# Routing terms and group deviations held in accumulator banks, image edges cleared in pairs: attention and conditional convolution on one core

## The chip, the cores and the metric

The kernel runs on one core of one Trainium2 chip. The metric is device microseconds of one execution; the time given is the median of several runs. The engines are named as in the profile: PE (TensorE: matrix products and transposes into accumulator banks, PSUM), DVE (VectorE), ACT (ScalarE), POOL (GpSimd) and SP (SyncE, which issues all DMAs). Each works through its own list in order and waits for the others by semaphores. SBUF is the memory of ordinary tensors.

## What is computed

For each of 16 images of 128 channels and 32 x 32 pixels, in float32:

```
x = x + attention(groupnorm(x))       # 4 heads of 32, softmax over d for q, over n for k
y = groupnorm(x)                      # 32 groups of 4 channels
pooled = mean of y over 4 x 4 cells                      # (128, 16)
r = relu(rconv_w . pooled + rconv_b)                     # 16 x 16 = 256 routing terms
g = sigmoid(relu(fc_w . r + fc_b))                       # 3 experts x 128 input channels
w = sum over k of g[k] * expert_weight[k]                # a filter of this image's own
out = x + conv3x3(y, w)                                  # padding of 1
```

## The kernel before

One image takes the whole 128 partitions as channels; the work of six images overlaps as a pipeline. Time goes in steps t, one per image: `run_steps` (line 333) runs steps -1 to 8 and 15 to 20 written out, and 9 to 14 as a loop of two steps. Each engine has a function `step` with its order of parts written by hand; `do(part, t, p, age)` calls a part for image t - age, `turn` the same for the group statistics, where one turn serves the first norm of image j and the second norm of image j - 3 together (`GAP = 3`, two columns). Buffers with index p alternate between even and odd images.

The parts that the change and the prediction touch, in the order of one image's flow:

- Group statistics, tensors of two columns. DVE's bn_aggr gives mean and variance per channel (`meanvar`). PE's `group_means` (L1211) averages the means over groups into `ps_stat`, a bank of 512 columns. DVE's `means` (L824) stores the negated mean (`nmean`), `differences` (L829) adds it to the channel mean (`dev`), `squared_differences` (L836) squares it (`dev_sq`), `spreads` (L843) adds the variance (`spread`). PE's `group_variances` (L1216) averages that, DVE's `variances` (L850) reads it back, POOL takes the power -0.5.
- DVE's `context_mask` (L955), `mix_start` (L949, `mix_base`) and `mix_evacuate` (L964, `mix`) stand behind `spreads`; PE's `outputs` (L1289) needs `mix`.
- Routing. POOL multiplies the pooled values by `rconv_t` (L534). PE's `routing` (L1302) sums them over channels into columns 0 to 255 of `ps_stat`. DVE's `route_bias` (L1032) adds the bias and stores `route_y` in SBUF, column 256 of which is a constant one; `route_sums` (L1043) makes, per expert, the relu of `route_y` times a row of `fc`, summed. Then `route_relu` (L1051), the gates, `filters_second` and `filters_third` (L1082, L1089) mix the expert filters into `w_full`.
- ACT rounds `w_full` to `w_hi` (L700), POOL computes the rest `w_lo` (L544); so too `img_hi`/`img_lo` for pixels. Each tap of the convolution (L1357) makes three products, hi x hi, hi x lo and lo x hi.
- SP copies the images by one column to left and right (L402 to L406). POOL's `image_edges` (L548) waits for all four copies and clears the column that wrapped around, by one instruction for each of the four, before `filters_low` (`w_lo`).
- POOL's `normalise1` (L492) writes `x`, `low1` (L499) `x_lo`, `x_scale` (L511) scales `x_nt`.
- PE's `keep_busy` (L1309) puts products whose result is not used (fillers, L1318, into columns 256 to 511 of `ps_stat`) into steps 1 to 3.

`ps_stat` is shared, so PE waits before it writes there: `group_means` and `keep_busy` wait until the routing terms of an earlier image were taken out (`route_y_done`). DVE's `step` sets the order of all this:

```
turn(means, t, p, 0)
do(k_sums, t, p, 2)
turn(differences, t, p, 0)
do(memory_scale, t, p, 2)
turn(squared_differences, t, p, 0)
```

Of the kernel before, what the change touches and what calls it, by code (L numbers as in the profile page):

```python
# [25 lines left out]
def attention_condconv_kernel(  # L26
# [38 lines left out]
    with ctx:  # L65
# [12 lines left out]
        zeros = sb("zeros", [128, H])  # L78
# [34 lines left out]
        dev_sq = sb("dev_sq", [128, 2])  # L113
# [49 lines left out]
        route_y = sb("route_y", [128, RF + 1])  # L163
# [15 lines left out]
        left_hi = [sb(f"left_hi{p}", [128, H, W], F32R) for p in range(2)]  # L179
        left_lo = [sb(f"left_lo{p}", [128, H, W], F32R) for p in range(2)]  # L180
        right_hi = [sb(f"right_hi{p}", [128, H, W], F32R) for p in range(2)]
        right_lo = [sb(f"right_lo{p}", [128, H, W], F32R) for p in range(2)]
# [11 lines left out]
        ps_stat = psum("ps_stat", [128, 512])  # L194

# [177 lines left out]
        def _(sp):  # L373
# [22 lines left out]
            def flat(img):  # L396
                return img[:, :, :].bitcast(F32).rearrange("p h w -> p (h w)")

            def shift_images(b, p):

                sp.wait_ge(img_hi_done, b + 1)
                sp.dma_start(flat(left_hi[p])[:, 1:N], flat(img_hi[p])[:, 0:N - 1]).then_inc(shifted[p], 16)  # L402
                sp.dma_start(flat(right_hi[p])[:, 0:N - 1], flat(img_hi[p])[:, 1:N]).then_inc(shifted[p], 16)
                sp.wait_ge(img_lo_done, b + 1)
                sp.dma_start(flat(left_lo[p])[:, 1:N], flat(img_lo[p])[:, 0:N - 1]).then_inc(shifted[p], 16)
                sp.dma_start(flat(right_lo[p])[:, 0:N - 1], flat(img_lo[p])[:, 1:N]).then_inc(shifted[p], 16)  # L406
# [35 lines left out]
        def _(pool):  # L442
# [7 lines left out]
            nc.gpsimd.memset(route_y[:, RF:RF + 1], 1.0)  # L450
# [97 lines left out]
            def image_edges(b, p):  # L548
                pool.wait_ge(shifted[p], 32 * (b - p) + 64)
                for img, column in ((left_hi, 0), (left_lo, 0), (right_hi, W - 1), (right_lo, W - 1)):  # L550
                    last = nc.gpsimd.tensor_tensor(img[p][:, :, column:column + 1], zeros[:, :].unsqueeze(2), zeros[:, :].unsqueeze(2), ALU.add)  # L551
                last.then_inc(edges_done, 1)
# [215 lines left out]
        def _(dve):  # L768
            v = nc.vector
            def constants():  # L770
# [10 lines left out]
                v.tensor_copy(memv_t[:, :], ps_att[0:MEM, 128:256])  # L781
# [13 lines left out]
            def memory_mix():  # L795
                dve.wait_ge(setup_pe, 5)
                v.tensor_copy(mem_mix[:, :], ps_att[:, 128:256]).then_inc(setup_dve, 1)
# [28 lines left out]
            def differences(j, p):  # L826
                dve.wait_ge(nmean_done, j + 1)
# [642 lines left out]
```

## Time and profile before

| | us |
|---|---|
| median of 3 runs | 441.21 (437.83 to 441.52) |
| profiled execution | 440.93 |
| its span, first to last instruction | 439.2 |
| PE busy | 414.9 (94%) |
| DVE busy | 359.6 (82%) |
| ACT busy | 303.1 (69%) |
| POOL busy | 262.4 (60%) |

All durations below come from the one profiled execution, taken by the hardware's profiler. PE is matrix products, PEld the loading of their weights, which overlaps them. Products are pipelined and their ends are modelled, so a busy PE is not a PE at its peak. A row of a timeline begins with the start (us from the start of the span) and the duration; `x16` is the count, and in brackets stand the idle time ahead of the first and who ended it. Durations of neighbouring rows overlap a little, since an engine takes up an instruction before the last one has ended. Waits are inferred from semaphore events; "issue" is time without a wait that the profile shows.

### The profile page before, as it was taken

To read this page: it belongs to the slowest core of one execution; us is meant where nothing else is said; L and a number is where in the kernel's file an instruction comes from. 1 tells how busy PE (TensorE), PEld (TensorE's weight loads), DVE (VectorE), ACT (ScalarE), POOL (GpSimd) and SP (SyncE) were. 2 spreads that over 40 slices of the span, in tenths; PEclk is the share of its full clock that TensorE was granted. 3 is DMA by queue.
4 is the path that set the end of the run, shared out by engine and by line. 5 is a ranking of instruction groups with operands and counts; after the bars stand their busy time and mean duration, and the time that the engine had idled before them with its cause. 6 is when DMAs were issued, how large, how long until landed. Compare 5 with 4: busy or idle time off the path is not lost.

```text
span 439.2 us, 8966 instructions
## 1 busy us (share of the span) xinstructions
PE 414.9 (94%) x2575; PEld 360.5 (82%) x2575; DVE 359.6 (82%) x778; ACT 303.1 (69%) x942; POOL 262.4 (60%) x245
## 2 busy tenths in 40 slices
PE   6888798999999999999999999999999999999987
PEld 5887687978888788979898888879798988778777
DVE  4574989798998989898989999898989798997540
ACT  2586685769695887868695959778686968654131
POOL 4646465749394957768494948576584849252330
PEclk8699998999999999999999999999999999999999
DMA  6420224324435151626253351606262422424331
GB/s 191 182 98 2 96 98 147 143 95 171 166 128 209 65 229 43 242 96 241 96 198 140 126 208 57 261 16 239 95 239 96 180 108 96 193 96 193 142 147 48
DMA packets 19078, 61.64 MB, mean 140 GB/s; under 512 B 3025, under 2 KB 4321, under 8 KB 19041
## 3 DMA queue, kind: packets, MB, share of 16 engines
q1 hardware_dynamic: 19040, 61.21, 37.0%
q8 instruction: 16, 0.26, 0.2%
q14 instruction: 22, 0.17, 0.1%
HBM read 19.29 MB, written 8.39 MB: 63 GB/s over the span
## 4 chain that ended last, share of the span: by engine, by line
PE 42%; DVE 22%; issue 16%; ACT 13%; POOL 3%; DMA 3%; DVEq 1%; ACTq 0%; SPq 0%
PE ps_conv L1357 15%; PE ps_y L1289 6%; PE ps_att L1257 5%; DVE w_full L1089 4%; ACT expert_raw L694 4%; DVE q_exp L912 3%; DMA xa<-in_x_dram 3%; DVE route_terms L1043 3%; PE ps_y L1279 3%; POOL w_lo L544 2%; ACT qk L608 2%; ACT squares L581 2%; PE ps_qkv L1238 2%; ACT x_hi L598 2%; PE ps_qkv L1239 2%
## 5 line engine op out<-in xcount | busy, mean ns | idle before, releaser
L608 ACT ACTIVATE qk<-ps_qkv,scale 128x256 f32<-128x256 f32 x128 | 54.3, 470 | 8.0 <-PE ps_qkv L1240 4.3
L700 ACT ACTIVATE w_hi<-w_full 128x1152 fp32r<-128x1152 f32 x16 | 18.7, 1168 | 54.7 <-DVE w_full L1095 54.7
L551 POOL TENSOR_TENSOR left_hi<-zeros 128x32 fp32r<-128x32 f32 x16 | 8.5, 529 | 79.8 <-DMA right_lo<-img_lo 79.8
L544 POOL TENSOR_TENSOR w_lo<-w_full,w_hi 128x1152 fp32r<-128x1152 f32 x16 | 42.7, 2670 | 12.9 <-ACT w_hi L700 8.0
L499 POOL TENSOR_TENSOR x_lo<-x,x_hi 128x1024 fp32r<-128x1024 f32 x16 | 38.4, 2397 | 14.1 <-ACT x_hi L598 14.1
L1238 PE MATMUL ps_qkv<-wqk_hi,x_hi 128*128 128x256 f32 x128 | 41.5, 324 | 1.8 <-ACT qk L608 1.8
L525 POOL TENSOR_TENSOR scale<-ssq,minus_half 128x8 f32<-128x8 f32 x16 | 26.2, 1638 | 28.4 <-DVE ssq L970 28.4
L667 ACT ACTIVATE y_scaled<-ps_y 128x128 f32<-128x128 f32 x128 | 33.3, 292 | 12.0 <-PE ps_y L1289 12.0
L1357 PE MATMUL ps_conv<-img_hi,w_hi 128*128 128x512 f32 (+1 forms) x96 | 37.4, 404 | 3.7 <-POOL w_lo L544 2.1
L1357 PE MATMUL ps_conv<-left_lo,w_hi 128*128 128x512 f32 (+2 forms) x96 | 40.6, 424 | 0.0
L1357 PE MATMUL ps_conv<-right_hi,w_hi 128*128 128x512 f32 (+2 forms) x96 | 38.0, 397 | 0.0
L1357 PE MATMUL ps_conv<-right_hi,w_lo 128*128 128x512 f32 (+2 forms) x96 | 38.0, 396 | 0.0
L1357 PE MATMUL ps_conv<-left_hi,w_hi 128*128 128x512 f32 (+2 forms) x96 | 37.2, 388 | 0.0
L1357 PE MATMUL ps_conv<-left_hi,w_lo 128*128 128x512 f32 (+2 forms) x96 | 37.0, 387 | 0.0
L1357 PE MATMUL ps_conv<-right_lo,w_hi 128*128 128x512 f32 (+2 forms) x96 | 37.0, 386 | 0.0
L1239 PE MATMUL ps_qkv<-wqk_lo,x_hi 128*128 128x256 f32 x128 | 36.6, 286 | 0.0
L1240 PE MATMUL ps_qkv<-wqk_hi,x_lo 128*128 128x256 f32 x128 | 36.5, 285 | 0.0
L1357 PE MATMUL ps_conv<-img_hi,w_lo 128*128 128x512 f32 (+1 forms) x96 | 36.2, 388 | 0.0
L1357 PE MATMUL ps_conv<-img_lo,w_hi 128*128 128x512 f32 (+1 forms) x96 | 35.7, 386 | 0.0
L1257 PEld LDWEIGHTS ps_att<-x_nt,k_exp 128*128 128x128 f32 x256 | 30.3, 190 | 6.4 <-ACT k_exp L634 6.0
L1257 PE MATMUL ps_att<-x_nt,k_exp 128*128 128x130 f32 x256 | 32.3, 278 | 2.7 <-ACT k_exp L634 2.1
L581 ACT ACTIVATE squares<-ps_qkv 128x128 f32<-128x128 f32 x128 | 33.3, 282 | 0.8 <-PE ps_qkv L1223 0.8
(176 smaller groups left out, 1342.5 us busy)
## 6 DMA issues: line engine op xcount, KB each, us to landing
xa<-in_x_dram SPq DMA_DIRECT2D x16, 512.0 KB, 4.0
xb<-in_x_dram SPq DMA_DIRECT2D x16, 512.0 KB, 4.7
left_hi<-img_hi SPq DMA_DIRECT2D x16, 511.5 KB, 3.0
right_hi<-img_hi SPq DMA_DIRECT2D x16, 511.5 KB, 4.1
left_lo<-img_lo SPq DMA_DIRECT2D x16, 511.5 KB, 2.9
right_lo<-img_lo SPq DMA_DIRECT2D x16, 511.5 KB, 3.7
out_dram<-expert_raw SPq DMA_DIRECT2D x15, 512.0 KB, 2.9
expert_raw<-_conv_expert_weight_dram SPq DMA_DIRECT2D x1, 1728.0 KB, 9.1
```

What stands on the lines that cost most here:

```text
L499: nc.gpsimd.tensor_tensor(x1_lo[:, :], x1[:, :], x1_hi[:, :].bitcast(F32), ALU.subtract).then_inc(x1_lo_done, 1)
L525: nc.gpsimd.tensor_tensor(scale2[:, :], ssq2[:, :], minus_half[:, :], ALU.pow).then_inc(scale2_done, 1)
L544: nc.gpsimd.tensor_tensor(w_lo[p][:, :, :].rearrange("p t o -> p (t o)"), w_full[:, :], w_hi[p][:, :, :].bitcast(F32).rearrange("p t o -> ...
L581: last = nc.scalar.activation(squares[:, tile(t)], ps_qkv[h][:, tile(t % (NT // 2))], ACT.Square, accum_out=ssq1_sum[:, t:t + 1])
L608: nc.scalar.activation(qk[:, t, :], ps_qkv[t % 2][:, 0:QK], ACT.Copy, scale=scale1[:, t:t + 1]).then_inc(qkv_done, 1)
L667: last = nc.scalar.activation(y_scaled[:, t, :], ps_y[:, tile(t)], ACT.Square, accum_out=ssq2_sum[:, t:t + 1])
L1238: mm(o, x1_hi[:, tile(t)], wqk_hi[:, :], start=True, stop=False)
L1239: mm(o, x1_hi[:, tile(t)], wqk_lo[:, :], start=False, stop=False)
L1240: mm(o, x1_lo[:, tile(t)], wqk_hi[:, :], start=False, stop=True).then_inc(qkv_ps, 1)
L1257: last = mm(ps_att[:, 0:CEXT], k_exp[:, t, :], x_nt[p][:, t, :], start=(t == 0), stop=(t == NT - 1))
L1289: last = mm(ps_y[:, tile(t)], q_t[p][:, tile(t)], mix[p][:, :], start=True, stop=True)
L1357: last = mm(into, weight[:, tap, :], pixels[:, top + down:bottom + down, :], start=(n == 0 and part == 0), stop=(n == TAPS - 1 and part == 2))
```

## The change

`route_y` and `dev_sq` become columns of `ps_stat` (0 to 256, and 4 to 5), so `route_bias` adds the bias in place and `route_sums` reads the bank. `differences` subtracts `ps_stat` itself and moves ahead of `means`. PE waits for `route_sum_done` where it waited for `route_y_done`, and the fillers leave out columns 256 and 257. The column of ones is set by DVE once, ahead of the first `route_bias`, instead of by POOL. The four shifted copies become two tensors with hi and lo side by side, and `image_edges` clears each with one instruction of 64 elements.

```
-        dev_sq = sb("dev_sq", [128, 2])
-        route_y = sb("route_y", [128, RF + 1])
+        dev_sq = ps_stat[:, 4:6]
+        route_y = ps_stat[:, 0:RF + 1]
...
-        left_hi = [sb(f"left_hi{p}", [128, H, W], F32R) for p in range(2)]
...
+        left = [sb(f"left{p}", [128, 2, H, W], F32R) for p in range(2)]
+        right = [sb(f"right{p}", [128, 2, H, W], F32R) for p in range(2)]
+        left_hi, left_lo = ([left[p][:, k, :, :] for p in range(2)] for k in range(2))
...
             def image_edges(b, p):
                 pool.wait_ge(shifted[p], 32 * (b - p) + 64)
-                for img, column in ((left_hi, 0), (left_lo, 0), (right_hi, W - 1), (right_lo, W - 1)):
-                    last = nc.gpsimd.tensor_tensor(img[p][:, :, column:column + 1], zeros[:, :].unsqueeze(2), zeros[:, :].unsqueeze(2), ALU.add)
-                last.then_inc(edges_done, 1)
+                blank = zeros[:, :].rearrange("p (k h w) -> p k h w", k=2, w=1)
+                nc.gpsimd.tensor_tensor(left[p][:, :, :, 0:1], blank, blank, ALU.add)
+                nc.gpsimd.tensor_tensor(right[p][:, :, :, W - 1:W], blank, blank, ALU.add).then_inc(edges_done, 1)
...
             def differences(j, p):
-                dve.wait_ge(nmean_done, j + 1)
+                dve.wait_ge(gmean_ps, j + 1)
+                if past(j, 1):
+                    dve.wait_ge(dev_sq_done, j)
                 c = columns(j)
-                v.tensor_tensor(dev[:, c], meanvar[:, c, 0], nmean[p][:, c], ALU.add).then_inc(dev_done, 1)
+                v.tensor_tensor(dev[:, c], meanvar[:, c, 0], ps_stat[:, c], ALU.subtract).then_inc(dev_done, 1)
...
             def route_bias(b, p):
...
+                if not past(b, 1):
+                    v.memset(route_y[:, RF:RF + 1], 1.0)
...
             def route_sums(b, p):
...
-                    last = v.scalar_tensor_tensor(route_terms[:, k, :], route_y[:, :], 0.0, fc[:, k, :], ALU.max, ALU.mult,
+                    last = v.scalar_tensor_tensor(route_terms[:, k, :], route_y, 0.0, fc[:, k, :], ALU.max, ALU.mult,
...
             def step(t, p):
...
+                turn(differences, t, p, 0)
                 turn(means, t, p, 0)
                 do(k_sums, t, p, 2)
-                turn(differences, t, p, 0)
...
             def group_means(j, p):
...
-                    pe.wait_ge(route_y_done, j - GAP)
+                    pe.wait_ge(route_sum_done, j - GAP)
...
             def keep_busy(t, place):
...
-                    pe.wait_ge(route_y_done, turns - GAP)
+                    pe.wait_ge(route_sum_done, turns - GAP)
                 for _ in range(IDLE_PRODUCTS[place][t]):
-                    mm(ps_stat[:, 256:512], wqk_hi[:, 0:128], wqk_hi[:, :], start=True, stop=True)
+                    mm(ps_stat[:, 258:512], wqk_hi[:, 0:128], wqk_hi[:, 0:254], start=True, stop=True)
```

Two set-up tensors move to other columns of another bank (`ps_att`), which leaves their work as it was.

On DVE, step 3, before the change: the group deviations, what stands behind them up to `mix`, and the routing of image 0.

```order
L941 TENSOR_TENSOR mem_scale<-mem_factor,k_rsum 128x1
L836 TENSOR_TENSOR dev_sq<-dev 128x2
L1018 TENSOR_SCALAR pooled_c<-pooled,nmean 128x16
L843 TENSOR_TENSOR spread<-dev_sq,meanvar 128x2
L955 TENSOR_TENSOR context<-ps_att,head_mask 128x128
L949 SCALAR_TENSOR_TENSOR mix_base<-mem_mix,mem_scale,bias_share 128x128
L850 TENSOR_SCALAR gvar<-ps_stat 128x2
L964 SCALAR_TENSOR_TENSOR mix<-ps_att,k_rsum,mix_base 128x128
L805 BN_STATS stats<-xa 128x6 x2
L1032 TENSOR_TENSOR route_y<-ps_stat,rconv_bias 128x256
L1043 SCALAR_TENSOR_TENSOR route_terms,route_sum<-route_y,fc 128x257 x3
```

The same place in the changed kernel:

```order
L944 TENSOR_TENSOR mem_scale<-mem_factor,k_rsum 128x1
L839 TENSOR_TENSOR ps_stat<-dev 128x2
L1021 TENSOR_SCALAR pooled_c<-pooled,nmean 128x16
L846 TENSOR_TENSOR spread<-ps_stat,meanvar 128x2
L958 TENSOR_TENSOR context<-ps_att,head_mask 128x128
L952 SCALAR_TENSOR_TENSOR mix_base<-mem_mix,mem_scale,bias_share 128x128
L853 TENSOR_SCALAR gvar<-ps_stat 128x2
L967 SCALAR_TENSOR_TENSOR mix<-ps_att,k_rsum,mix_base 128x128
L806 BN_STATS stats<-xa 128x6 x2
L1036 MEMSET ps_stat 128x1
L1037 TENSOR_TENSOR ps_stat<-ps_stat,rconv_bias 128x256
L1048 SCALAR_TENSOR_TENSOR route_terms,route_sum<-ps_stat,fc 128x257 x3
```

The order is the same but for the memset, which stands at image 0 alone; the operands in `ps_stat` are what is new.

On POOL, one image before: the edges (`left_hi` to `right_lo`, from `zeros`) between the scale of the second norm and the low part of the filters.

```order
L525 TENSOR_TENSOR scale<-ssq,minus_half 128x8
L551 TENSOR_TENSOR left_hi<-zeros 128x32
L551 TENSOR_TENSOR left_lo<-zeros 128x32
L551 TENSOR_TENSOR right_hi<-zeros 128x32
L551 TENSOR_TENSOR right_lo<-zeros 128x32
L544 TENSOR_TENSOR w_lo<-w_full,w_hi 128x1152
```

And in the changed kernel:

```order
L526 TENSOR_TENSOR scale<-ssq,minus_half 128x8
L552 TENSOR_TENSOR left<-zeros 128x64
L553 TENSOR_TENSOR right<-zeros 128x64
L545 TENSOR_TENSOR w_lo<-w_full,w_hi 128x1152
```

Four instructions of 32 elements became two of 64; nothing else on POOL has moved.

## Rows read from the trace of the kernel before

**Rows 1.** Stretches: length, busy PE, PEld, DVE, ACT, POOL (instructions), clock, DMA share, GB/s.
```profile
183.65:207.90 24.25, 23.74 (x149) 20.56 (x148) 22.10 (x47) 18.50 (x58) 16.86 (x14) 1.00 0.39 149
207.90:231.70 23.80, 23.72 (x149) 20.46 (x148) 21.77 (x47) 18.46 (x58) 15.82 (x14) 1.00 0.42 160
```

**Rows 2.** Waits, whole span: us in total, times, longest us.
```profile
PEld ps_y L1295 <- DVE y_scaled L977: 8.4, 15, 1.0
PEld ps_att L1257 <- ACT k_exp L634: 6.0, 10, 1.4
...
PEld ps_conv L1357 <- POOL w_lo L544: 2.8, 4, 1.2
```

**Rows 3.** Chain that ended last, one image: start us, us, what.
```profile
181.24 0.53 PE ps_stat L1302 x2
...
182.84 0.78 DVE route_terms L1043 x5
...
195.96 1.58 PE ps_conv L1357 x6
```

**Rows 4.** Timeline of DVE, the routing of one image.
```profile
181.79 0.42 DVE L1032 TENSOR_TENSOR route_y<-ps_stat,rconv_bias 128x256 f32<-128x256 f32 x1 [0.24 <-PE ps_stat L1302]
182.25 0.67 DVE L1043 SCALAR_TENSOR_TENSOR route_terms<-route_y,fc 128x257 f32<-128x257 f32 x1
...
182.84 0.42 DVE L1043 SCALAR_TENSOR_TENSOR route_terms<-route_y,fc 128x257 f32<-128x257 f32 x1
```

**Rows 5.** Timeline of POOL, the same image.
```profile
181.44 1.20 POOL L492 TENSOR_SCALAR x<-xa,rstd,shift 128x1024 f32<-128x1024 f32 x1 [0.24 <-POOL shift L483]
...
191.48 1.23 POOL L551 TENSOR_TENSOR left_lo<-zeros 128x32 fp32r<-128x32 f32 x1
...
193.05 2.66 POOL L544 TENSOR_TENSOR w_lo<-w_full,w_hi 128x1152 fp32r<-128x1152 f32 x1
```

**Rows 6.** Groups by line: busy us, mean ns of one, idle time ahead, releaser.
```profile
L544 POOL TENSOR_TENSOR w_lo<-w_full,w_hi 128x1152 fp32r<-128x1152 f32 x16 | 42.7, 2670 | 12.9 <-ACT w_hi L700 8.0 <-issue 4.9
...
L499 POOL TENSOR_TENSOR x_lo<-x,x_hi 128x1024 fp32r<-128x1024 f32 x16 | 38.4, 2397 | 14.1 <-ACT x_hi L598 14.1
...
L1043 DVE SCALAR_TENSOR_TENSOR route_terms<-route_y,fc 128x257 f32<-128x257 f32 x48 | 21.1, 488 | 0.5
...
L905 DVE TENSOR_REDUCE q_max<-qk 128x32 f32<-128x1024 f32 x16 | 19.4, 1212 | 0.0
...
L1032 DVE TENSOR_TENSOR route_y<-ps_stat,rconv_bias 128x256 f32<-128x256 f32 x16 | 6.8, 425 | 16.9 <-PE ps_stat L1302 16.9
...
L870 DVE TENSOR_TENSOR k_quarter<-k_half 128x256 f32<-128x256 f32 x16 | 6.7, 421 | 0.0
```

**Rows 7.** Line L1043: duration in ns, least, median and greatest; first and last start.
```profile
L1043 DVE SCALAR_TENSOR_TENSOR route_terms<-route_y,fc x48: 414/419/1032, 60.8 to 416.4; 128x257 f32<-128x257 f32 x48
```

**Rows 8.** Timeline of DVE, step 2.
```profile
34.54 1.82 DVE L843 TENSOR_TENSOR spread<-dev_sq,meanvar 128x1 f32<-128x1 f32 x1
...
36.48 0.34 DVE L949 SCALAR_TENSOR_TENSOR mix_base<-mem_mix,mem_scale,bias_share 128x128 f32<-128x128 f32 x1
```

**Rows 9.** Timeline of PE, step 2.
```profile
36.41 0.38 PE L1216 MATMUL ps_stat<-spread,group_avg 128*128 128x1 f32 x2 [1.65 <-DVE spread L843]
```

**Rows 10.** Timeline of PE, step 3.
```profile
60.92 1.90 PE L1318 MATMUL ps_stat<-wqk_hi 128*128 128x256 f32 x14
63.40 0.38 PE L1238 MATMUL ps_qkv<-wqk_hi,x_hi 128*128 128x256 f32 x1 [0.58 <-ACT qk L608]
```

**Rows 11.** Timeline of POOL, image 6, behind its edges.
```profile
216.89 2.67 POOL L544 TENSOR_TENSOR w_lo<-w_full,w_hi 128x1152 fp32r<-128x1152 f32 x1 [1.32 <-ACT w_hi L700]
```

**Rows 12.** Timeline of PE, image 14.
```profile
409.07 0.50 PE L1357 MATMUL ps_conv<-img_hi,w_hi 128*128 128x512 f32 x1 [0.91 <-POOL w_lo L544]
```

**Rows 13.** Stretches of PE alone: length, busy (instructions), clock, DMA share, GB/s.
```profile
69.59:73.00 3.41, 1.74 (x11) 1.00 0.00 0
73.00:76.41 3.41, 3.17 (x12) 0.51 0.41 113
```

More of the change, by code:

```diff
@@ L77, in attention_condconv_kernel @@
         ones = sb("ones", [128, 128])
-        zeros = sb("zeros", [128, H])
+        zeros = sb("zeros", [128, 2 * H])
         group_avg = sb("group_avg", [128, 128])
@@ L176, in attention_condconv_kernel @@
         img_lo = [sb(f"img_lo{p}", [128, H, W], F32R) for p in range(2)]
-        left_hi = [sb(f"left_hi{p}", [128, H, W], F32R) for p in range(2)]
-        left_lo = [sb(f"left_lo{p}", [128, H, W], F32R) for p in range(2)]
-        right_hi = [sb(f"right_hi{p}", [128, H, W], F32R) for p in range(2)]
-        right_lo = [sb(f"right_lo{p}", [128, H, W], F32R) for p in range(2)]
+        left = [sb(f"left{p}", [128, 2, H, W], F32R) for p in range(2)]
+        right = [sb(f"right{p}", [128, 2, H, W], F32R) for p in range(2)]
+        left_hi, left_lo = ([left[p][:, k, :, :] for p in range(2)] for k in range(2))
+        right_hi, right_lo = ([right[p][:, k, :, :] for p in range(2)] for k in range(2))
         spare = expert_raw[:, :, :].rearrange("o k f -> o (k f)")
@@ L396, in flat @@
             def flat(img):
-                return img[:, :, :].bitcast(F32).rearrange("p h w -> p (h w)")
+                return img.bitcast(F32).rearrange("p h w -> p (h w)")
             def shift_images(b, p):
                 sp.wait_ge(img_hi_done, b + 1)
-                sp.dma_start(flat(left_hi[p])[:, 1:N], flat(img_hi[p])[:, 0:N - 1]).then_inc(shifted[p], 16)
-                sp.dma_start(flat(right_hi[p])[:, 0:N - 1], flat(img_hi[p])[:, 1:N]).then_inc(shifted[p], 16)
+                sp.dma_start(flat(left_hi[p])[:, 1:N], flat(img_hi[p][:, :, :])[:, 0:N - 1]).then_inc(shifted[p], 16)
+                sp.dma_start(flat(right_hi[p])[:, 0:N - 1], flat(img_hi[p][:, :, :])[:, 1:N]).then_inc(shifted[p], 16)
                 sp.wait_ge(img_lo_done, b + 1)
-                sp.dma_start(flat(left_lo[p])[:, 1:N], flat(img_lo[p])[:, 0:N - 1]).then_inc(shifted[p], 16)
-                sp.dma_start(flat(right_lo[p])[:, 0:N - 1], flat(img_lo[p])[:, 1:N]).then_inc(shifted[p], 16)
+                sp.dma_start(flat(left_lo[p])[:, 1:N], flat(img_lo[p][:, :, :])[:, 0:N - 1]).then_inc(shifted[p], 16)
+                sp.dma_start(flat(right_lo[p])[:, 0:N - 1], flat(img_lo[p][:, :, :])[:, 1:N]).then_inc(shifted[p], 16)
             def load_constants():
@@ L449, in _ @@
                 nc.gpsimd.memset(x_nt[p][:, :, C:CEXT], 1.0)
-            nc.gpsimd.memset(route_y[:, RF:RF + 1], 1.0)
             nc.gpsimd.memset(ones[:, :], 1.0).then_inc(pool_zeros, 1)
@@ L780, in constants @@
                 v.tensor_copy(wout_t[:, :], ps_att[:, 0:C])
-                v.tensor_copy(memv_t[:, :], ps_att[0:MEM, 128:256])
+                v.tensor_copy(memv_t[:, :], ps_att[0:MEM, 384:512])
                 v.tensor_scalar(bias_share[:, :], bias_raw[:, :], 1.0 / HEADS, None, ALU.mult)
@@ L796, in memory_mix @@
                 dve.wait_ge(setup_pe, 5)
-                v.tensor_copy(mem_mix[:, :], ps_att[:, 128:256]).then_inc(setup_dve, 1)
+                v.tensor_copy(mem_mix[:, :], ps_att[:, 256:384]).then_inc(setup_dve, 1)
             def gn1_stats(b, p):
@@ L1169, in constants @@
                 tr(ps_att[:, 0:C], wout_raw[:, :], ident[:, :])
-                tr(ps_att[0:MEM, 128:256], mem_c[:, 1, :], ident[:, :]).then_inc(setup_pe, 1)
+                tr(ps_att[0:MEM, 384:512], mem_c[:, 1, :], ident[:, :]).then_inc(setup_pe, 1)
                 pe.wait_ge(gvar_done, 1)
@@ L1183, in memory_mix @@
                 pe.wait_ge(setup_dve, 6)
-                mm(ps_att[:, 128:256], mem_context[:, :], wout_t[:, :], start=True, stop=True).then_inc(setup_pe, 1)
+                mm(ps_att[:, 256:384], mem_context[:, :], wout_t[:, :], start=True, stop=True).then_inc(setup_pe, 1)
             def expert_transpose(n):
```

## The prediction

> **What bounds the kernel now.** Read first the busy time by stretch, cut where route_zr ends [rows 1]: over one image of the steady state (23.8 us, or 24.3 every so often) PE is busy 23.7 us and DVE some 22, and no other engine is near that. PE looks full, but its ends are modelled, so the list of waits is read next [rows 2]: PE's weight loads still wait for DVE's y_scaled (8.4 us over 15 images), for k_exp (6.0 over 10) and for w_lo (2.8 over 4). That is about 0.5 us per image that PE can give back in the quick periods, and more in the longer ones. Then the chain that ended last, over one image [rows 3]: it leaves PE with the routing product, runs through DVE's route_y and route_terms and on through gates, mixed filters and DVE's long row of operations, and enters PE again at a convolution product that had waited for w_lo. So the period is a ring: a stretch of PE in its fixed order up to the routing product, and a stretch of DVE from route_y until PE has to wait for y_scaled, k_exp or w_lo. Whatever shortens the DVE stretch shortens the period while those waits last. Finally the timelines show what is odd in that stretch: the first of three equal route_terms takes 0.67 us and the second 0.42 [rows 4], while POOL runs the normalisation x from 181.44 to 182.64 [rows 5]. route_y, which takes one operand from the accumulators, ran its 0.42 us under the same x unhindered. An operation with both operands in SBUF was held back and one with a single one was not: the change acts on just that.
>
> **Routing terms.** route_terms has a median of 419 ns [rows 7]. In eleven images (2 to 12) the first one is like the row at 182.25, 0.67 us, so each loses 0.25: 11 x 0.25 = 2.7 us. Image 0 has the longest of all, 1032 ns [rows 7], 0.61 too much. (The mean of 488 over 48 [rows 6] holds the same: 48 x 0.069 = 3.3.) After the change route_terms has only fc in SBUF, as route_y has only the bias, so I expect 420 to 430 ns each. What follows moves forward with it: route_zr, ACT's gate, w_first, w_second, w_full, then y_scaled, k_exp, w_hi and w_lo. PE's waits for these are longer than 0.25 us together, so all of it reaches the end: **-2.7 us, and -0.6 for image 0**. The xa load that DVE's stats wait for is released by ACT operations behind the same ring, so it moves too.
>
> What does touching the accumulators cost? For reading, the nearest rows are equal work: 256 elements out of ps_stat (L1032) 425 ns, 256 between SBUF tensors (L870) 421 [rows 6]: 4 ns, taken as nothing. The Trainium skill speaks against this: "VectorE: DVE Perf Modes", The TRN2 errata, gives an operation from PSUM a fixed cost of 120 cycles where one from SBUF has 58, some 65 ns at 0.96 GHz; with five such operations per image that would be an estimated 5.2 us and eat the whole gain. The 4 ns of the two rows do not agree with that, and the measurement decides. For writing, no row has DVE do it. The low end is a small gain, the same 4 ns; the high end is that route_y, which now reads and writes one bank, goes at half its rate: (1212 - 421) / 768 = 1.03 ns per element [rows 6], 256 of them 0.26 us per image, 16 x 0.26 = 4.2 us. I take zero, as reading costs nothing extra, and keep 4.2 for the range.
>
> **Deviations.** dev now reads ps_stat, comes ahead of means and doesn't wait for it; nmean comes one slot (about 0.1 us) later, and its readers (the centre on DVE, image_high on ACT, shift1 on POOL) stand later than that anyway: nothing. dev_sq keeps two SBUF operands and writes PSUM; spread has one operand left in SBUF. In steady state neither is held up, so nothing changes. Step 2 is different: there spread took 1.82 us, at a time when POOL scaled x_nt [rows 8], and PE waited 1.65 for it [rows 9]. The stall itself goes, but not its worth. Two places behind spread stands mix_base, again with two SBUF tensors, and it is now the one that meets x_nt: it cannot run before x_nt lets go, about 0.15 us before spread's end, 36.36 - 0.15 = 36.2, and ends near 36.55 instead of 36.82; mix follows, now without a wait of its own of 0.2. PE's outputs, which need mix, gain about **0.5 us**, not 1.65. If dev_sq should be caught as well, the 0.5 is lost.
>
> **Edges.** An edge instruction of 32 elements takes a slot of 0.20 us. For 64, POOL's slope from w_lo and x_lo, (2670 - 2397) / 128 = 2.1 ns per element [rows 6], adds 0.07: two slots of 0.27 instead of four of 0.20, 0.26 saved per image. In ten images this is hidden: w_lo waits for w_hi, 1.32 us after the last edge in the row at 216.89 [rows 11], and both move together. In four (3, 5, 7, 12) the shift DMAs land later, the edges fall among DVE operations with two SBUF operands, one edge is held up, for 1.23 us in the image shown [rows 5], and those left behind it delay w_lo, for which PE then waits. One edge fewer behind the held one is worth 0.25 us: **-1.0 us**. In image 14 the edges end after w_hi and PE waits 0.91 for w_lo [rows 12]: **-0.25**. Image 15 needs w_lo late: nothing.
>
> **New waits and small things.** PE's group product and its fillers now wait for route_sum_done instead of route_y_done. For the group product that is a step old. At step 3, 14 fillers start at 60.92, right behind route_y [rows 10]; they now wait for all three route_terms, to about 61.95. Behind them on PE stands a projection which until now waited for ACT and began at 63.40; fillers of some 1.7 us end near 63.6 now, 0.2 late, but ACT wants its result only after w_first. So nothing on the path, and a new pause of PE of one microsecond. A memset on DVE, once, ahead of route_y of image 0: +0.1. Fillers of 254 columns and the longer zeros: nothing.
>
> **Sum.** 2.7 + 0.6 + 0.5 + 1.0 + 0.25 - 0.1 = 4.95 us. The profiled execution took 440.93 (439.2 span and 1.7 around it), which gives 436.0; it is 0.3 under the median of the three runs, 441.21, so for the median I say **436.2 us**.
>
> **Rivals.** (a) PE becomes the bound and half of the steady gain stays behind. For it: 23.72 us of PE in a period of 23.80 [rows 1]. Against it: y_scaled and k_exp are still waited for in most images [rows 2]. Half of 2.7 and of 1.0 remains: 441.2 - 3.1 = 438.1. (b) The change does what it says, but touching the accumulators costs what it saves: route_y at half rate, +4.2, gives 440.4. For it: no row has DVE write there. A fixed cost per operation out of PSUM would do the same; by the page named above, 441.4. (c) Slower: reading and writing in one bank slows not only route_y but the three route_terms too, each by 0.26 us. That is 4 x 0.26 = 1.06 us per image at the head of the DVE stretch, 16.9 us in all, 453.1. It decides from (445.6 - 436.2) / 16 = 0.59 us per image on. Against it: route_y out of ps_stat runs at the SBUF rate [rows 6]. (d) More gain: PE ran from 73.0 to 76.4 us at half clock (1.2 GHz), after a stretch in which it was busy 1.74 of 3.41 us [rows 13]. With step 2 and image 0 shorter the pauses fall elsewhere. If that stretch goes, half of the 3.17 us of work in it comes back, 1.5 us: 434.7; the new pause at 61 us could as well bring one on, 437.7.
>
> **How the numbers follow.** A measurement here can tell about 1% from no change, that is below 436.8 or above 445.6. Forecast 0.55 (434.8 to 437.7; of it 0.42 below 436.8), (d) with more gain 0.08, (a) 0.18, (b) 0.12, (c) 0.07. Faster 0.42 + 0.08 = 0.50; same 0.13 + 0.18 + 0.12 = 0.43; slower 0.07. The three runs lie 3.7 us apart, which the edges must allow for: 432.8 (the gain of (d) and a run 2 us low) to 440.9 (into (b)).
>
> **What would show it.** Right: all 48 route_terms at 415 to 430 ns, also those under x; route_y near 425; spread at step 2 about 0.15 and mix_base there held up in its place; two edges of about 0.3 us in undisturbed images; smaller waits of PE for y_scaled and k_exp; periods of 23.5 and 23.8 us in place of 23.8 and 24.3. Wrong: route_y or route_terms above 500 ns; periods unchanged with PE's waits gone (rival a); a held DVE operation elsewhere that takes the 0.25 us.

## The result, and the profile after

The changed kernel takes **435.82 us** (median of 8 runs, 434.8 to 436.8) beside 440.58 for the kernel before: a ratio of 0.9899, 95% interval [0.9876, 0.9923]. A second series of 6 runs gave 435.36 and 0.9887 [0.986, 0.9915]. The forecast was 436.2, inside 432.8 to 440.9.

The profiled execution has a span of 434.8 us against 439.2. Cut where `route_zr` ends, the 4.4 us lie here: 1.43 up to image 0 (62.74 against 61.31), 0.92 between images 0 and 1 (25.35 against 24.43), 2.02 over the thirteen periods behind, from image 1 to image 14 (311.06 against 309.04), 0.06 in the tail. (The expectations below speak of the same sums as fourteen periods; they are thirteen.) The forecast had 3.7 in these periods.

The stretches that answer to [rows 1]: length, busy PE, PEld, DVE, ACT, POOL, clock, DMA share, GB/s.

```profile
180.91:205.13 24.22, 23.83 (x148) 20.48 (x147) 22.03 (x48) 18.50 (x58) 15.49 (x12) 1.00 0.40 150
205.13:228.78 23.65, 23.55 (x148) 20.40 (x147) 21.50 (x48) 18.49 (x58) 17.05 (x12) 1.00 0.41 159
```

The two shown went from 24.25 to 24.22 and from 23.80 to 23.65. Over the thirteen, most quick ones fell from 23.8 to between 23.55 and 23.75, and the long ones from 24.2 to 24.4 to between 24.0 and 24.2. PE's waits, to be laid beside [rows 2]:

```profile
PEld ps_y L1300 <- DVE y_scaled L980: 7.6, 15, 0.9
PEld ps_att L1262 <- ACT k_exp L635: 6.9, 13, 1.4
...
PEld ps_stat L1221 <- DVE spread L846: 3.0, 7, 0.8
...
PEld ps_conv L1362 <- POOL w_lo L545: 2.0, 5, 0.9
```

y_scaled and w_lo fell by 0.8 each, k_exp rose. The third line is the one to stop at. Before, PE's weight loads waited for spread 4 times (3.9 us, the longest 1.9, that of step 2); now 7 times, none over 0.8. Of the 4 before one lay in the thirteen periods, of the 7 now three do. A wait that I had put into step 2 alone has come into the steady state.

The durations (least, median, greatest in ns) that answer to [rows 7] and to the groups in [rows 6]:

```profile
L1048 DVE SCALAR_TENSOR_TENSOR route_terms<-ps_stat,fc x48: 419/422/429, 60.0 to 411.9; 128x257 f32<-128x257 f32 x48
...
L1037 DVE TENSOR_TENSOR ps_stat<-ps_stat,rconv_bias x16: 416/432/433, 59.5 to 410.8; 128x256 f32<-128x256 f32 x16
...
L839 DVE TENSOR_TENSOR ps_stat<-dev x19: 168/170/172, 6.6 to 408.2; 128x2 f32<-128x2 f32 x13, 128x1 f32<-128x1 f32 x6
```

All 48 route_terms are short. Before, 12 of the 48 started while x ran, and these 12 alone took 0.66 us or more; now 23 start under x, and none is long. One image's terms under POOL's x, on DVE and then on POOL, where before the first took 0.67 us [rows 4, 5]:

```profile
179.11 0.43 DVE L1037 TENSOR_TENSOR ps_stat<-ps_stat,rconv_bias 128x256 f32<-128x256 f32 x1 [0.95 <-PE ps_stat L1307]
179.58 0.43 DVE L1048 SCALAR_TENSOR_TENSOR route_terms<-ps_stat,fc 128x257 f32<-128x257 f32 x1
...
179.93 0.42 DVE L1048 SCALAR_TENSOR_TENSOR route_terms<-ps_stat,fc 128x257 f32<-128x257 f32 x1
```

```profile
178.76 1.20 POOL L493 TENSOR_SCALAR x<-xa,rstd,shift 128x1024 f32<-128x1024 f32 x1 [0.24 <-POOL shift L484]
```

Step 2 on DVE, on POOL and on PE, which answers to [rows 8, 9]:

```profile
34.21 0.16 DVE L846 TENSOR_TENSOR spread<-ps_stat,meanvar 128x1 f32<-128x1 f32 x1
...
34.48 1.73 DVE L952 SCALAR_TENSOR_TENSOR mix_base<-mem_mix,mem_scale,bias_share 128x128 f32<-128x128 f32 x1
...
36.34 0.35 DVE L967 SCALAR_TENSOR_TENSOR mix<-ps_att,k_rsum,mix_base 128x128 f32<-128x128 f32 x1
```

```profile
34.16 1.90 POOL L512 TENSOR_TENSOR x_nt<-x_nt,scale 128x1024 f32<-128x1024 f32 x1
```

```profile
34.42 0.38 PE L1221 MATMUL ps_stat<-spread,group_avg 128*128 128x1 f32 x2
...
36.74 1.05 PE L1294 MATMUL ps_y<-mix,q_t 128*128 128x128 f32 x7 [0.91 <-DVE mix L967]
```

x_nt runs to 36.06. spread, with one SBUF operand left, passes under it; mix_base, with two, is held to 36.2 in its place. For the gain, two more rows of the kernel before, on POOL and on DVE:

```profile
34.45 1.90 POOL L511 TENSOR_TENSOR x_nt<-x_nt,scale 128x1024 f32<-128x1024 f32 x1
```

```profile
37.16 0.35 DVE L964 SCALAR_TENSOR_TENSOR mix<-ps_att,k_rsum,mix_base 128x128 f32<-128x128 f32 x1 [0.17 <-PE ps_att L1271]
```

x_nt shows that this execution was 0.29 us ahead before step 2 began to differ. Less that, the product behind spread came 1.7 us sooner (34.42 against 36.41), but mix, and with it PE's outputs, only 0.53 (36.34 against 37.16). The forecast had 0.5; the expectations below put it at 0.7.

Step 3 on PE, beside [rows 10]:

```profile
61.25 1.88 PE L1323 MATMUL ps_stat<-wqk_hi 128*128 128x254 f32 x14 [1.08 <-DVE route_terms L1048]
62.97 0.28 PE L1243 MATMUL ps_qkv<-wqk_hi,x_hi 128*128 128x256 f32 x1
```

The new pause is there, 1.08 us, and the projection behind it lost nothing.

### The profile page after: what moved, and what is told of

Its sections match the earlier page's. It is cut to its first block, busy times and chain, and to the rows that moved or that the text cites. A ratio compares the mean times of both kernels' runs of the same rounds, so it can differ in the third digit from the quotient of the medians.

```text
span 434.8 us, 8952 instructions
## 1 busy us (share of the span) xinstructions
PE 412.7 (95%) x2575; PEld 358.3 (82%) x2575; DVE 354.5 (82%) x779; ACT 303.1 (70%) x942; POOL 260.6 (60%) x212
## 4 chain that ended last, share of the span: by engine, by line
PE 50%; DVE 21%; issue 14%; ACT 10%; POOL 2%; DMA 1%; DVEq 1%; ACTq 0%; POOLq 0%
PE ps_conv L1362 20%; PE ps_y L1294 6%; PE ps_att L1262 6%; DVE w_full L1094 4%; ACT expert_raw L695 3%; PE ps_y L1284 3%; DVE q_exp L915 3%; PE ps_qkv L1243 2%; DVE route_terms L1048 2%; PE ps_qkv L1245 2%; PE ps_qkv L1244 2%; ACT x_hi L599 2%; ACT qk L609 2%; PE ps_stat L1307 2%; POOL w_lo L545 2%
## 5 line engine op out<-in xcount | busy, mean ns | idle before, releaser
L1362 PE MATMUL ps_conv<-left,w_hi 128*128 128x512 f32 (+2 forms) x192 | 70.0, 404 | 0.0
L1362 PE MATMUL ps_conv<-right,w_hi 128*128 128x512 f32 (+2 forms) x192 | 61.2, 391 | 0.0
L552 POOL TENSOR_TENSOR left<-zeros 128x64 fp32r<-128x64 f32 x16 | 6.3, 394 | 79.7 <-DMA right<-img_lo 79.7
L1362 PEld LDWEIGHTS ps_conv<-right,w_hi 128*128 128x128 f32 x192 | 35.2, 188 | 6.5
L1362 PEld LDWEIGHTS ps_conv<-left,w_hi 128*128 128x128 f32 x192 | 35.5, 189 | 4.6
L1362 PE MATMUL ps_conv<-right,w_lo 128*128 128x512 f32 (+2 forms) x96 | 37.8, 395 | 0.0
L1362 PE MATMUL ps_conv<-left,w_lo 128*128 128x512 f32 (+2 forms) x96 | 37.0, 387 | 0.0
L1362 PE MATMUL ps_conv<-img_hi,w_lo 128*128 128x512 f32 (+1 forms) x96 | 36.2, 387 | 0.0
```

Of the source, the lines that this page charges most:

```text
L1362: last = mm(into, weight[:, tap, :], pixels[:, top + down:bottom + down, :], start=(n == 0 and part == 0), stop=(n == TAPS - 1 and part == 2))
```

## The experiments

**Each part of the change alone, and the change without its edges.** Four kernels on one chip, beside 440.32 us for the kernel before.

The routing terms alone:

```
+        route_y = ps_stat[:, 0:RF + 1]
-                    last = v.scalar_tensor_tensor(route_terms[:, k, :], route_y[:, :], 0.0, fc[:, k, :], ALU.max, ALU.mult,
+                    last = v.scalar_tensor_tensor(route_terms[:, k, :], route_y, 0.0, fc[:, k, :], ALU.max, ALU.mult,
-                    pe.wait_ge(route_y_done, j - GAP)
+                    pe.wait_ge(route_sum_done, j - GAP)
```

> The kernel before with the routing terms alone in the accumulator bank (and with them the fillers of 254 columns, the column of ones set by DVE, and PE's waits for route_sum_done). Theory (a DVE operation with two SBUF operands is held up by POOL's x, one with a single SBUF operand is not): all 48 route_terms at 415 to 430 ns, quick periods 23.55 us instead of 23.8, and 2.5 to 3.5 us less than before, about 437.5. Rival (the gain comes from the edges): 48 route_terms short, but the time within 0.5 us of before. Rival (the gain is the stretch at half clock that the changed kernel's profile lacks): under 1 us where that stretch is still there.

Measured: 438.14 us, ratio 0.9951 [0.9928, 0.9973]. The thirteen periods take 308.65 us, 2.4 less; all 48 terms are short:

```profile
L1044 DVE SCALAR_TENSOR_TENSOR route_terms<-ps_stat,fc x48: 418/422/428, 61.3 to 413.3; 128x257 f32<-128x257 f32 x48
```

This part alone carries nearly half of the gain: 2.2 us by the medians. In the profiles, image 1's `route_zr` ends 0.6 us earlier than before and the thirteen periods take 2.4 less, near the 0.6 and 2.7 in the sum.

The edges alone, two instructions of 64 for four of 32:

```
+                nc.gpsimd.tensor_tensor(left[p][:, :, :, 0:1], blank, blank, ALU.add)
+                nc.gpsimd.tensor_tensor(right[p][:, :, :, W - 1:W], blank, blank, ALU.add).then_inc(edges_done, 1)
```

> The kernel before with the edges alone cleared in pairs. The prediction's term: 1.25 us less than before, 439.3, with w_lo 0.25 us earlier in the images whose edges come late. Theory after the changed kernel's profile, where the second edge was held for 1.0 to 2.2 us in six images: the pairs are caught between DVE's operations as often as the four, and the time stays within 0.5 us of before. Rival (the gain comes from the edges): 3 us or more less.

Measured: 439.51 us, 0.9988 [0.9966, 1.001]: 0.5 to 0.8 us, not told from nothing.

The deviations alone:

```
+        dev_sq = ps_stat[:, 4:6]
+                turn(differences, t, p, 0)
                 turn(means, t, p, 0)
                 do(k_sums, t, p, 2)
-                turn(differences, t, p, 0)
```

> The kernel before with the group deviations alone in the accumulator bank and taken ahead of the means. Theory: spread at step 2 takes 0.16 us instead of 1.82, mix_base there 1.7 instead of 0.34, and 0.5 us less than before, 440.1; steady periods as before (23.8 and 24.3). Rival (the whole stall of 1.65 us comes back): 439.0.

Measured: 440.13 us, 1.0013 [0.9992, 1.0034]: no gain at all. The gain in step 2 is there (spread takes 0.16 us at 33.24, mix_base 1.75 behind it), but the thirteen periods rose from 311.06 to 313.05. Something in the steady state eats what step 2 gives.

The changed kernel with four edge instructions again:

```
+                for img, column in ((left_hi, 0), (left_lo, 0), (right_hi, W - 1), (right_lo, W - 1)):
+                    last = nc.gpsimd.tensor_tensor(img[p][:, :, column:column + 1], zeros[:, 0:H].unsqueeze(2), zeros[:, 0:H].unsqueeze(2), ALU.add)
```

> The changed kernel with four edge instructions of 32 elements again, on the same tensors. The prediction's term: 1.25 us more than the changed kernel, 437.1. Theory after the changed kernel's profile: within 0.5 us of it, 435.3 to 436.3. Rival (the gain comes from the edges): 439 or more.

Measured: 436.59 us, 0.9933 [0.9908, 0.9958], 0.8 over the changed kernel's first series and 1.2 over its second; the intervals overlap. What an edge costs is seen on POOL. First the changed kernel, then the one with four, image 6 of both:

```profile
211.71 0.31 POOL L552 TENSOR_TENSOR left<-zeros 128x64 fp32r<-128x64 f32 x1 [4.78 <-DMA right<-img_lo]
211.96 2.09 POOL L553 TENSOR_TENSOR right<-zeros 128x64 fp32r<-128x64 f32 x1
214.00 2.67 POOL L545 TENSOR_TENSOR w_lo<-w_full,w_hi 128x1152 fp32r<-128x1152 f32 x1
```

```profile
210.57 2.30 POOL L552 TENSOR_TENSOR left<-zeros 128x32 fp32r<-128x32 f32 x2 [4.77 <-DMA right<-img_lo]
212.83 0.44 POOL L552 TENSOR_TENSOR right<-zeros 128x32 fp32r<-128x32 f32 x2
213.22 2.67 POOL L545 TENSOR_TENSOR w_lo<-w_full,w_hi 128x1152 fp32r<-128x1152 f32 x1
```

In both an edge is held for 2.1 us, until DVE's subtraction with two SBUF operands (q_exp, 1.22 us) is through. With two, w_lo follows at once and starts 0.25 us behind w_hi's end; with four, two edges stand between and it starts 0.59 behind. Held images come in every kernel, but not the same ones: 3, 5, 7, 12 before; 1, 2, 6, 8, 10, 11, 12 after; 0, 6, 10, 12 with four. Summed over images 1 to 14, w_lo starts 4.97 us behind w_hi before, 3.59 with the edges alone, 3.72 in the changed kernel (4.09 in its second profile), 4.23 with four. But it is 3.56 with the routing terms alone, whose edges are those of before, so this sum doesn't tell two instructions from four.

The parts alone don't add up to the whole. By the medians they gain 2.2, 0.8 and 0.2 us, 3.2 together (by the ratios 2.1), and the whole 4.8 (4.4). In the thirteen periods the terms (2.41 less) and the deviations (1.99 more) do add up: the changed kernel with four edges holds both and takes 0.53 less. The edges are what differs, 0.25 alone and 1.49 on top of the others. Since two profiles of one and the same kernel differ by up to 1.6 us there (below), what the edges are worth stays open.

**Is it x running beside route_terms?** The kernel before with POOL's x held until the routing sums are done; nothing in the accumulators.

```
+                if past(b, 3):
+                    pool.wait_ge(route_sum_done, b - 2)
                 pool.wait_ge(shift1_done, b + 1).then_inc(x1_started, 1)
```

> Before, with one wait more: from image 3 on GpSimd's normalisation x starts only when the routing sums of the image two before are done. Nothing moves to the accumulators. Theory (the first route_terms loses 0.25 us in eleven images because x, running beside it, holds back an operation with two SBUF operands): the first route_terms takes 0.42 to 0.43 us from image 3 on, only image 0 and perhaps 2 stay long; the fourteen periods of the steady state, 311.06 us before and 308.65 with the routing terms alone in the accumulators, fall to about 309, and the median is some 2 us under the kernel before. Rival (the accumulators are what makes it short, not x's absence): the first ones stay at 0.66 and the time does not fall. Second rival (x later costs as much on its own way to the projections as it saves): route_terms short, the time within 0.5 us of before, and new waits of PE for x_hi or of ScalarE behind x. On the clock: spread of step 2 is still held for 1.8 us here, so if that hold is what brings on a half-clock stretch later, one of 3 to 4 us is seen between 30 and 80 us; if such stretches fall by chance, it may be absent.

Measured: 449.28 us, 1.0219 [1.0184, 1.0253]. The durations of the terms (as above), and one line of the waits:

```profile
L1045 DVE SCALAR_TENSOR_TENSOR route_terms<-route_y,fc x48: 419/421/431, 60.7 to 425.2; 128x257 f32<-128x257 f32 x48
```

```profile
PE ps_att L1248 <- DVE k_max_part L878: 10.2, 15, 1.2
```

None of the 48 starts under x here, and all are short, with both operands in SBUF. So the overlap is the cause, and the accumulators are one way out of it. The second rival named the price but not its size: x waited 34.6 us for them over 13 images, 2.7 in each, what comes from it came later, and PE now stands for k_max_part (2.3 us in all before), so that the time rose by 9.1 us. Waiting was a far dearer way out.

**What makes the steady state of the deviations slower?** Here is the chain from one group statistic to the next on DVE, first before, then after:

```profile
104.98 0.15 DVE L824 TENSOR_SCALAR nmean<-ps_stat 128x2 f32<-128x2 f32 x1
105.05 0.15 DVE L934 RECIPROCAL k_rsum<-k_den 128x1 f32<-128x1 f32 x1
105.17 0.16 DVE L829 TENSOR_TENSOR dev<-meanvar,nmean 128x2 f32<-128x2 f32 x1
105.28 0.16 DVE L941 TENSOR_TENSOR mem_scale<-mem_factor,k_rsum 128x1 f32<-128x1 f32 x1
105.38 0.16 DVE L836 TENSOR_TENSOR dev_sq<-dev 128x2 f32<-128x2 f32 x1
...
105.67 0.15 DVE L843 TENSOR_TENSOR spread<-dev_sq,meanvar 128x2 f32<-128x2 f32 x1
```

```profile
102.56 0.14 DVE L832 TENSOR_TENSOR dev<-meanvar,ps_stat 128x2 f32<-128x2 f32 x1
102.62 0.15 DVE L825 TENSOR_SCALAR nmean<-ps_stat 128x2 f32<-128x2 f32 x1
102.73 0.16 DVE L937 RECIPROCAL k_rsum<-k_den 128x1 f32<-128x1 f32 x1
102.93 0.16 DVE L944 TENSOR_TENSOR mem_scale<-mem_factor,k_rsum 128x1 f32<-128x1 f32 x1
103.01 0.17 DVE L839 TENSOR_TENSOR ps_stat<-dev 128x2 f32<-128x2 f32 x1
...
103.29 0.15 DVE L846 TENSOR_TENSOR spread<-ps_stat,meanvar 128x2 f32<-128x2 f32 x1
```

Before, dev stood between k_rsum and mem_scale, which needs k_rsum: that pair lay 0.23 us apart with work in between. After, mem_scale follows k_rsum directly and still lies 0.20 behind it, with nothing in between; dev is early, but its successor stands behind them all the same. From the row's first start to that of spread it was 0.69 us and is 0.73, and from PE's mean products (104.56 and 102.10) to spread 1.11 and 1.19. (The two orders of step 3 under "The change" begin at mem_scale, behind this place, and so don't show the move.) PE stands at exactly that point, and two tiny products show it:

```profile
106.00 0.28 PE L1216 MATMUL ps_stat<-spread,group_avg 128*128 128x2 f32 x2
```

```profile
103.54 0.34 PE L1221 MATMUL ps_stat<-spread,group_avg 128*128 128x2 f32 x2
```

Adding, over the thirteen periods, the times between successive starts on PE: from the first to the second spread product 0.63 us before, 1.33 after; from the product ahead of them 3.79 and 4.06; from the last output to the routing sum behind 1.62 and 1.90. That is 1.25 us, and 1.15 in the kernel with the deviations alone (1.20, 4.13, 1.86). To try it, the changed kernel with that one move undone:

```
-                turn(differences, t, p, 0)
                 turn(means, t, p, 0)
                 do(k_sums, t, p, 2)
+                turn(differences, t, p, 0)
```

> The changed kernel, with one thing undone: the deviations are again issued between k_rsum and mem_scale instead of ahead of the means; they still read the accumulators. Theory (placed first, they no longer stand between pairs of instructions that depend on each other: mem_scale follows k_rsum after 0.20 instead of 0.11 us, spread starts 1.16 instead of 1.08 us after the second mean product, and PE, which stands at the spread product, waits 0.05 to 0.08 us more in each of 14 images, 1.33 instead of 0.63 us between the two spread products and 0.3 ahead of the first): those two sums return to 0.63 and 3.79, the steady periods fall by about 1 us to 308, step 2 keeps its gain, and the median is 0.7 to 1.2 us under the changed kernel. Rival (what is lost there comes back at the next wait of PE, for y_scaled or k_exp, since DVE's stretch sets the period): the two sums return, the time does not move by more than 0.3 us. Second rival (dev_sq in the accumulators itself makes spread late): the sums stay.

Measured: 434.59 us, 0.9891 [0.986, 0.9923]. The three sums are 0.63, 3.87 and 1.60, the thirteen periods 307.37 us. And the deviations alone, in their old place:

> The kernel before with the deviations alone in the accumulators, and issued where they stood, between k_rsum and mem_scale. Theory (the deviations gain 0.7 us in step 2, take a half-clock stretch between 30 and 80 us away with it, and lose some 1.2 us again in the steady state only because they were moved ahead of the means): the sums of PE at the spread products stay at before's 0.63 and 3.8 us where the deviations alone in their new place had 1.20 and 4.13, no half-clock stretch between 30 and 80 us, and the median is 1 to 2 us under the kernel before, 438 to 439. Rival (writing the squares to the accumulators makes spread late by itself, and the order is without effect): the sums are 1.2 and 4.1 again, and the time is that of before. Second rival (clock stretches fall by chance): the sums stay, a stretch may be there, and the gain is 0 to 0.7 us.

Measured: 438.89 us, 0.9965 [0.9945, 0.9984], where the same accumulators with the move gave 1.0013 [0.9992, 1.0034]: the intervals don't meet. The sums are 0.61, 3.98 and 1.63, the periods 310.36 us; spread starts 1.05 us behind the mean products. By the medians the move costs 1.2 us, by the ratios 2.1. In all six kernels with the move the first of the three sums is 1.20 to 1.37 us, in the eight without it 0.59 to 0.79. So the move, not the accumulators, made PE wait. Nor is it the clock: among the executions whose granted clock was full on the mean (0.999 or more), the deviations alone with the move have a median of 439.7 us (6 executions), the kernel before beside them 437.8 (4).

**Better versions.** The hi edges of both sides cleared by one instruction as soon as the hi shifts have landed, the lo edges by another, so that one stands ahead of w_lo; and that with the old order of the deviations:

```
+            def image_edges_high(b, p):
+                pool.wait_ge(shifted_hi[p], 16 * (b - p) + 32)
+                clear_edges(sides_hi[p])
...
+                do(image_edges_high, t, p, 5)
                 do(image_edges, t, p, 5)
```

> The changed kernel, with the edges in another pairing: the two hi edges are cleared by one instruction as soon as the two hi shifts have landed, the two lo edges by a second one when the lo shifts have landed, so one instruction instead of two stands between the last landing and w_lo. Theory (the second edge, which in seven images is held for 1.0 to 2.2 us beside DVE's work with two SBUF operands, is what makes w_lo start 0.1 to 0.25 us later than w_hi alone would allow, and four edges cost 0.8 us in all): w_lo follows w_hi's end by 0.13 to 0.26 us in most images, PE's waits for w_lo fall from 2.9 us to under 2, and the median is 0.3 to 1.0 us under the changed kernel. Rival (the held edge is hidden behind w_hi anyway, and what counts is the late landing of a few images): within 0.3 us of the changed kernel. Clock: step 2 is as in the changed kernel (mix_base held, PE out 0.7 us earlier), so no half-clock stretch between 30 and 80 us.

> The changed kernel with both edits: hi edges early and the deviations back between k_rsum and mem_scale. Theory (two separate losses, at two places of PE's order): the gains of the two add up, 1.0 to 2.0 us under the changed kernel, some 434 us. Rival (both only give PE time that it loses again at y_scaled and k_exp): no better than the better of the two alone.

Measured: 434.27 us, 0.9874 [0.9843, 0.9906], and 435.32 us, 0.9896 [0.9865, 0.9928]. w_lo waits for w_hi again in the image shown above:

```profile
211.04 0.31 POOL L557 TENSOR_TENSOR sides_lo<-zeros 128x64 fp32r<-128x64 f32 x1 [4.16 <-DMA sides_lo<-img_lo]
213.30 2.67 POOL L546 TENSOR_TENSOR w_lo<-w_full,w_hi 128x1152 fp32r<-128x1152 f32 x1 [1.95 <-ACT w_hi L710]
```

In eleven of images 1 to 14 w_lo starts 0.13 to 0.22 us behind w_hi, as that theory said, and the sum is 2.88 us (3.00 and 3.12 in the two other profiles with early hi edges), below every kernel without them. By the medians the two gains did not add up, but the clock differed: five of the six executions with both edits had a mean clock of 0.988 to 0.992, where one of five and two of six had so with one edit. The sixth, at full clock, took 433.43 us; those with one edit at full clock took 434.02 to 434.90 and 433.49 to 434.95. So whether the gains add up is open. Then the changed kernel and its two edits side by side:

> The changed kernel itself, beside the two edits of it, on one chip. Theory: 436 us, a ratio of about 0.990 to before, no half-clock stretch between 30 and 80 us, and 309.0 us in the fourteen steady periods. Rival (its first runs fell low or high by a chip): more than 1 us from 435.8.

> The changed kernel with the deviations back between k_rsum and mem_scale, beside the changed kernel itself. Theory: 1 to 1.5 us under it (its first profile had 307.37 us in the fourteen periods against 309.04), some 434.6 us. Rival (the gain is handed back at PE's next waits): within 0.5 us of it.

> The changed kernel with the hi edges cleared early, beside the changed kernel itself. Theory: 0.5 to 1.5 us under it (first profile 308.07 us in the fourteen periods against 309.04), some 434.5 us. Rival (the edges are hidden behind w_hi but for a few images, whose landing decides): within 0.5 us of it.

Measured: 435.36 [0.986, 0.9915], 434.98 [0.9843, 0.9906] and 434.73 us [0.9845, 0.9904]. Both edits lie below the changed kernel, by 0.4 and 0.6 us, and neither is told from it: the three intervals overlap almost wholly. (Of the executions at full clock alone, four of each, the medians are 435.35, 434.89 and 434.33.) For the order the rival's 0.5 us was the nearer. The two profiles of one and the same kernel with the old order show where a microsecond can go. DVE's stats of one image, first profile, then second:

```profile
223.34 1.29 DVE L806 BATCH_NORM_STATS2 stats<-xa 128x6 f32<-128x512 f32 x2 [1.59 <-DMA xa<-in_x_dram]
```

```profile
224.86 1.29 DVE L806 BATCH_NORM_STATS2 stats<-xa 128x6 f32<-128x512 f32 x2 [2.58 <-DMA xa<-in_x_dram]
```

In the second the load of xa landed 1 us later after its issue, and that period took 24.57 us instead of 23.59. With that, and 0.59 more in the period behind image 1, the thirteen came to 308.94, nearly those of the changed kernel (309.22 beside it), though the three sums are as low here (0.62, 3.89 and 1.64).

**The clock.** The clock granted between 30 and 80 us, in one row each: before, the terms alone, the deviations alone in their old place, and the changed kernel (the clock is the third number from the end).

```profile
30.00:80.00 50.00, 42.10 (x312) 38.51 (x313) 39.57 (x79) 35.29 (x125) 31.07 (x25) 0.97 0.28 102
```

```profile
30.00:80.00 50.00, 42.09 (x314) 38.28 (x313) 39.35 (x80) 34.76 (x120) 29.56 (x24) 0.97 0.25 94
```

```profile
30.00:80.00 50.00, 42.22 (x320) 37.76 (x318) 40.16 (x80) 36.84 (x134) 32.85 (x24) 1.00 0.29 106
```

```profile
30.00:80.00 50.00, 43.02 (x329) 39.19 (x330) 40.05 (x89) 37.22 (x130) 31.50 (x25) 1.00 0.26 100
```

The 0.97 is a stretch of 3 to 4 us at half clock (1.2 GHz): at 73 us before, at 36 with the terms alone. All four kernels in which spread of step 2 is held for 1.8 us have one (the two shown, the edges alone, x later: 0.97 each); in the three others than before it began within 2 us of that wait of PE. All ten profiles in which spread passes have none. For four of these fourteen (x later, the hi edges early, the deviations in their old place, the changed kernel again) the expectations had it so.

That does not make the hold the cause in the kernel before. There the clock stayed full behind the hold, and the stretch at 73 us stands right behind other waits of PE, of which the first, for k_max_part, is the longest. PE ahead of the stretch and behind it, before:

```profile
70.53 0.33 PE L1246 MATMUL ps_att<-ident,k_max_part 128*128 128x128 f32 x1 [0.94 <-DVE k_max_part L876]
...
78.73 0.37 PE L1238 MATMUL ps_qkv<-wqk_hi,x_hi 128*128 128x256 f32 x1
```

And in the changed kernel:

```profile
69.01 0.33 PE L1251 MATMUL ps_att<-ident,k_max_part 128*128 128x128 f32 x1 [0.41 <-DVE k_max_part L879]
...
76.33 0.37 PE L1243 MATMUL ps_qkv<-wqk_hi,x_hi 128*128 128x256 f32 x1
```

With the routing terms alone this wait is 0.40, too; with the edges or the deviations alone it is 0.85 to 0.93, and no stretch follows it there. So each of the two pauses of PE was followed by a stretch in one execution and not in another, the change shortens both, and what decides is not shown. The price can be read: across the stretch the changed kernel's lead on PE grows from 1.52 us (70.53 less 69.01) to 2.40 (78.73 less 76.33), by 0.9, which is what the periods between images 0 and 1 differ by.

The mean granted clock of single executions tells how much of the whole gain may be the clock's. Of the 60 executions of the kernel before beside the experiments 6 ran at full clock throughout, with a median of 437.9 us, and of the 14 of the changed kernel 7, with 435.2. That leaves 2.8 us of the 4.8. So some 2 us of the measured gain, an estimate from few executions on more than one chip, go with half-clock stretches, which the changed kernel has more seldom.

## Why the prediction was right, and where it was not

- **Routing terms: right.** Cause and size: first terms of 0.43 us under x, 2.4 us in the steady state against 2.7, image 0's 1032 ns gone and 0.6 us with it. (By the medians of the terms alone it is 2.2 us in all, of 3.2.) That an operation with two SBUF operands is held by POOL and one with a single one isn't, was read from one row under x [rows 4, 5]; the run with x held back shows it from the other side. The Trainium skill, "SBUF — State Buffer", Who interferes with whom, says that a DVE instruction with at most one SBUF input, outside the 2-port modes, doesn't contend with GpSimd; the 48 terms agree. Of the 2-port modes it says that whichever issues first has the ports for its whole instruction. Carried over to two SBUF operands, that fits x_nt and mix_base; the held edge outlasted more than one of DVE's instructions, which no single "first" explains.
- **Accumulators: right to take them as nothing.** Writing costs 7 ns (432 against 425) and 9 (170 against 161), reading 3 (422 against 419): 0.02 to 0.03 us per image. The half rate kept for the range didn't come, nor did the rival that ended slower. The Trainium skill, "VectorE: DVE Perf Modes", The TRN2 errata, has 120 cycles for PSUM against 58 for SBUF, an estimated 65 ns more; that is not in these rows.
- **Step 2: right.** mix_base took the hold over, and 0.53 us were gained against the 0.5 in the sum. What the sum had at nothing is the half-clock stretch at 73 us: 0.9 us, which the forecast had only as a rival with 0.08 (and 1.5 us). The deviations alone, in their old place, gained 1.4 us in all.
- **Deviations in the steady state: wrong.** The step that failed reads "In steady state neither is held up, so nothing changes". It asked only whether an operand is held, and took the move ahead of means for a slot of 0.1 us that nobody waits for. The move took dev out from between two instructions that depend on each other, and PE waits at the end of that row in many images: 1.25 us in the three sums, and 1.99 over the thirteen periods with the deviations alone.
- **Edges: sum near, way off.** 1.25 us forecast; the single experiments give 0.5 (alone) to 1.2 (taken out again). But other images are held than before, and neither the times nor w_lo's lateness tell the pairs from the four; that one edge fewer behind the held one is what gains is not shown.
- **The sum** came out partly by luck. From profile to profile the gain of 4.43 us is 0.29 by which the execution was ahead of step 2 (in no term), 0.53 in step 2 (0.5 forecast), 0.61 up to image 0's routing (0.5 with the memset), 0.92 by the half-clock stretch (nothing), 2.02 in the thirteen periods (3.7) and 0.06 behind (0.25). So 1.9 us too little from image 1 on, of which the order is 1.25, is made up by 1.3 too much ahead of it, of which the clock is 0.9. The periods of 23.5 and 23.8 us that it named came to some 23.6 and 24.1.

Still open: how much of the move's 1.2 us the changed kernel gets back when it is undone (0.4 beside it on one chip, 1.2 between the two series); the landing of xa moves a single period by as much. Open too are what the edges are worth, and with them why the parts alone don't add up to the whole, and what brings a half-clock stretch on behind one pause of PE and not behind another.

## What to carry to other kernels

Where VectorE and GpSimd run side by side, count the SBUF operands of each VectorE instruction on the path: moving one into an accumulator bank costs a few ns and frees it, but the hold then falls on the next instruction with two, so look for that one before you price the gain. In a row of tiny dependent instructions the order is worth as much as their number: don't take an independent one from between two that depend on each other. And run each part of a change alone, and look at the clock of each execution, since a total that fits can hide a gain and a loss.

## What was not expected of the hardware

- A 32-element GpSimd edge of 0.25 us can be held for 2.1 us, past several DVE instructions; the one of 64 elements, 0.31 us, likewise.
- Small DVE instructions that don't depend on each other can start 0.06 us apart (102.56 and 102.62), a dependent one started 0.20 us after its predecessor (102.73 and 102.93): 0.14 us more, with no idle time shown in the rows.
- The same wait of 1.65 us of PE in step 2 was followed by a half-clock stretch within 2 us in three kernels, and by none in the kernel before, where one came behind shorter waits at 73 us. In the first 24 us such stretches come and go between executions of one kernel: the changed kernel's `route_zr` of image 0 ended at 61.31 us in one profile, with two such stretches, and at 59.59 in another, with none; the runs scatter by as much.
